# An attention-LSTM recurrence: 1/sum moved into the transposing product, and both gate products of a cell in one operation

## The reference

```python
def _lstm_cell(x, h, c, Wi, Wh, bi, bh):
    g = x @ Wi.T + bi + h @ Wh.T + bh
    i, f, gg, o = jnp.split(g, 4, axis=-1)
    c2 = jax.nn.sigmoid(f) * c + jax.nn.sigmoid(i) * jnp.tanh(gg)
    h2 = jax.nn.sigmoid(o) * jnp.tanh(c2)
    return (h2, c2)

def step(carry, x_t):
    h0, c0, h1, c1, a = carry
    xin = jnp.concatenate([x_t, a], axis=-1)
    h0, c0 = _lstm_cell(xin, h0, c0, Wi0, Wh0, bi0, bh0)
    h1, c1 = _lstm_cell(h0, h1, c1, Wi1, Wh1, bi1, bh1)
    q = h1 @ Wq.T
    attn = jax.nn.softmax(jnp.einsum('bh,bsh->bs', q, context), axis=-1)
    mixed = jnp.einsum('bs,bsh->bh', attn, context)
    a2 = jnp.tanh(jnp.concatenate([mixed, h1], axis=-1) @ Wo.T + bo)
    return ((h0, c0, h1, c1, a2), a2)
```

## Time and profile before

| | us |
|---|---|
| median of 3 runs | 1889.4 |
| lowest, highest | 1886.71, 1890.64 |
| the profiled execution | 1888.54 |
| its span, first to last instruction | 1886.8 |
| PE busy in the span | 1474.4 (78%) |
| DVE busy | 1174.6 (62%) |
| ACT busy | 760.2 (40%) |
| POOL busy | 207.7 (11%) |

### The profile page before, as it was taken

The page is one execution under the profiler, slowest core; times in us unless marked ns, Lnnn a source line. Parts: engine busy times, 40 slices in busy tenths (PEclk is TensorE's granted clock), DMA queues, the critical chain, the costliest instruction groups (busy, mean ns, idle before and its releaser), DMA issues. The chain is left out here.

```text
span 1886.8 us, 82660 instructions
## 1 busy us (share of the span) xinstructions
PE 1474.4 (78%) x34335; PEld 1282.6 (68%) x34336; DVE 1174.6 (62%) x4397; ACT 760.2 (40%) x1849; POOL 207.7 (11%) x427
## 2 busy tenths in 40 slices
PE   1557777777734999999999999999999783049997
PEld 0446666666623888888888888888888673026665
DVE  5878888888885556666666656666666484014444
ACT  2446666566554334444344444444344211013332
POOL 0000000000001000000000000000000002743333
PEclk9768888898856999999999999999999765569999
DMA  6000000000034000000000000000000160222222
GB/s 212 1 2 0 0 0 0 0 0 0 1 90 199 6 0 0 0 0 0 0 0 0 0 0 0 0 0 0 0 0 0 32 203 28 104 79 67 71 73 50
DMA packets 42813, 57.39 MB, mean 30 GB/s; under 512 B 5754, under 2 KB 32892, under 8 KB 40856
## 3 DMA queue, kind: packets, MB, share of 16 engines
q1 hardware_dynamic: 36672, 42.90, 7.5%
q0 software_dynamic: 5376, 12.66, 1.9%
q10 hardware_dynamic: 728, 1.34, 0.2%
HBM read 30.52 MB, written 26.88 MB: 30 GB/s over the span
## 5 line engine op out<-in xcount | busy, mean ns | idle before, releaser
L1517 DVE TENSOR_TENSOR hb<-psH,b_sb 128x512 f32<-128x512 f32 x72 | 49.8, 691 | 170.6 <-PE psH L1341 170.6
L900 PE MATMUL sc_a<-h_a,KH 128*128 128x48 f16 (+2 forms) x4096 | 124.2, 183 | 2.5 <-DVE h_a L1058 2.5
L900 PE MATMUL sc_b<-h_b,KH 128*128 128x48 f16 (+2 forms) x4096 | 123.0, 183 | 0.0
L860 PE MATMUL z_b<-h_b,WL 128*128 128x64 f16 x2304 | 112.2, 193 | 11.4 <-issue 3.0
L860 PE MATMUL z_a<-h_a,WL 128*128 128x64 f16 x2304 | 112.5, 194 | 9.3 <-DVE h_a L1050 1.8
L940 PEld LDWEIGHTS mx_a<-pmv_a,VH 128*128 128x128 f16 x4096 | 107.1, 96 | 16.4 <-DVE pmv_a L1086 16.1
L940 PEld LDWEIGHTS mx_b<-pmv_b,VH 128*128 128x128 f16 x4096 | 107.4, 96 | 15.9 <-DVE pmv_b L1086 15.9
L940 PE MATMUL mx_a<-pmv_a,VH 128*128 128x16 f16 x4096 | 113.2, 169 | 5.3 <-DVE pmv_a L1086 0.4
L940 PE MATMUL mx_b<-pmv_b,VH 128*128 128x16 f16 x4096 | 113.2, 170 | 5.0 <-DVE pmv_b L1086 0.3
L900 PEld LDWEIGHTS sc_a<-h_a,KH 128*128 128x128 f16 x4096 | 113.1, 96 | 2.6 <-DVE h_a L1058 2.6
L900 PEld LDWEIGHTS sc_b<-h_b,KH 128*128 128x128 f16 x4096 | 113.2, 96 | 0.0
(11 more groups left out here) (282 smaller groups left out, 3748.5 us busy)
## 6 DMA issues: line engine op xcount, KB each, us to landing
sorted_x<-zt SPq DMA_DIRECT2D x9, 1032.0 KB, 11.9
xr<-sorted_x SPq DMA_DIRECT2D x72, 65.0 KB, 1.8
xg<-sorted_x SPq DMA_DIRECT2D x72, 64.0 KB, 1.9
XT<-in_ctxT SPq DMA_DIRECT2D x1, 4096.0 KB, 13.1
x_scratch<-X SPq DMA_DIRECT2D x1, 4096.0 KB, 15.9
TOK<-x_scratch SPq DMA_DIRECT2D x4, 1024.0 KB, 10.2
w_sb<-in_w SPq DMA_DIRECT2D x1, 2048.0 KB, 12.8
b_sb<-in_b SPq DMA_DIRECT2D x1, 2048.0 KB, 19.8
```

The source lines that it names most:

```text
L860: mm = nc.tensor.matmul(q.z[layer][:, j * GB:(j + 1) * GB], WL[:, blk + j, w, :], mov[m], start=False, stop=False, skip_group_check=True)
L900: mm = nc.tensor.matmul(A.S[:, WIDE * n:WIDE * n + streamed(n)], KH[:, k, pair * P:(pair + 1) * P], A.h[1][:, 2 * n:2 * n + streamed(n) // ...
L1517: nc.vector.tensor_tensor(hb[:, u, :], psH[:, u, :], b1_sb[:, bass.ds(col, FF)], ALU.add).then_inc(v_hb, 1)
```

## The change

Three edits. The masked copy `pe` and its transposition are replaced: DVE writes two diagonal matrices, `dg[:, h, :]`, which are the constant `pick` (S at row s, column s where s has the parity h, else 0) times the reciprocal of each row; PE multiplies p, as the stationary operand of 64 x 64, with each of them and writes the two results to the lower and the upper 64 partitions. The first of the three own products is issued after the wait for `dg` and before this product; the other two stay where they were. The gate products: the cell state c becomes the fourth quarter of the gate tile, so that (i+1)g and (f+1)c are one operation of 128 columns. The tanh of the output gate gets a tile and an operation of its own, after the tanh of i, f, g. `pe`'s clearing is gone, and the count of the clearing semaphore is 16 instead of 18.

```diff
-                    nc.vector.tensor_reduce(par[:, 0:1], ident[0:64, 0:64:2], AX.X, ALU.add).then_inc(v_b, 1)
-                    nc.vector.tensor_reduce(par[:, 1:2], ident[0:64, 1:64:2], AX.X, ALU.add).then_inc(v_b, 1)
-                    dve.wait_ge(v_b, 3)
-                    nc.vector.tensor_scalar(pmask[:, :, :], par[:, :].unsqueeze(2).broadcast_to([64, 2, 64]),
-                                            S, None, ALU.mult).then_inc(v_b, 1)
+                    dve.memset(pick[:, :, :], 0.0).then_inc(v_b, 1)
+                    dve.wait_ge(v_b, 2)
+                    for h in range(2):
+                        nc.vector.tensor_scalar(pick[:, h, h::2], ident[0:64, h:64:2], S, None, ALU.mult).then_inc(v_b, 1)
...
                 q.gt = [sb(f"gt{l}_{t}", [P, 4, GB]) for l in range(2)]
+                q.c = [q.gt[l][:, 3, :] for l in range(2)]
+                q.og = [sb(f"og{l}_{t}", [P, GB]) for l in range(2)]
...
+                    def own_part(q, k):
+
+                        w, m = ((0, 0), (1, 0), (0, 1))[k]
+                        nc.tensor.matmul(q.Mv[:, :, :, 0], WO2[:, w, :],
+                                         q.h[1][:, 0:GB, m].rearrange("p (n b) -> p n b", b=2),
+                                         start=(k == 0), stop=False, skip_group_check=True)
...
-                            pe.wait_ge(A.s_pe, at + 1)
-                            nc.tensor.transpose(A.S[:, 128:256], A.pe[:, :], ident[:, :]).then_inc(A.s_pt, 1)
+                            pe.wait_ge(A.s_dg, at + 1)
+                            own_part(A, 0)
+                            for h in range(2):
+                                mm = nc.tensor.matmul(A.S[64 * h:64 * (h + 1), 128:192], A.p[:, :], A.dg[:, h, :],
+                                                      start=True, stop=True)
+                            mm.then_inc(A.s_pt, 1)
                             if not last:
                                 early0x(A, at + 1)
...
-                            for k, (w, m) in enumerate(((0, 0), (1, 0), (0, 1))):
-                                nc.tensor.matmul(A.Mv[:, :, :, 0], WO2[:, w, :],
-                                                 A.h[1][:, 0:GB, m].rearrange("p (n b) -> p n b", b=2),
-                                                 start=(k == 0), stop=False, skip_group_check=True)
+                            own_part(A, 1)
+                            own_part(A, 2)
...
-                            nc.scalar.activation(L.gt[l][:, :, :].rearrange("p g b -> p (g b)"), L.z[l][:, 0:4 * GB],
+                            nc.scalar.activation(L.gt[l][:, 0:3, :].rearrange("p g b -> p (g b)"), L.z[l][:, 0:3 * GB],
                                                  ACT.Tanh, scale=sc[:, I0 + l:I0 + l + 1]).then_inc(L.s_tg[l], 1)
+                            nc.scalar.activation(L.og[l][:, :], L.z[l][:, 3 * GB:4 * GB],
+                                                 ACT.Tanh, scale=sc[:, I0 + l:I0 + l + 1]).then_inc(L.s_to[l], 1)
...
-                            act.wait_ge(L.s_tg[l], lt + 1)
-                            nc.scalar.activation(L.os[l][:, :], L.gt[l][:, 3, :], ACT.Copy, scale=S / 2,
+                            act.wait_ge(L.s_to[l], lt + 1)
+                            nc.scalar.activation(L.os[l][:, :], L.og[l][:, :], ACT.Copy, scale=S / 2,
                                                  bias=S / 2).then_inc(L.s_os[l], 1)
...
-                        pool.memset(q.pe[:, :], 0.0).then_inc(s_zero, 1)
-                    pool.wait_ge(s_zero, 18)
+                    pool.wait_ge(s_zero, 16)
...
-                            nc.vector.scalar_tensor_tensor(L.u[l][:, 0, :], L.gt[l][:, 1, :], 1.0, L.c[l][:, :],
+                            nc.vector.scalar_tensor_tensor(L.u[l][:, :, :], L.gt[l][:, 0:2, :], 1.0, L.gt[l][:, 2:4, :],
                                                            ALU.add, ALU.mult).then_inc(L.s_uv[l], 1)
-                            nc.vector.scalar_tensor_tensor(L.u[l][:, 1, :], L.gt[l][:, 0, :], 1.0, L.gt[l][:, 2, :],
-                                                           ALU.add, ALU.mult).then_inc(L.s_uv[l], 1)
-                            dve.wait_ge(L.s_uv[l], 2 * lt + 2)
-                            nc.vector.scalar_tensor_tensor(L.c[l][:, :], L.u[l][:, 0, :], 0.5, L.u[l][:, 1, :],
+                            dve.wait_ge(L.s_uv[l], lt + 1)
+                            nc.vector.scalar_tensor_tensor(L.c[l], L.u[l][:, 1, :], 0.5, L.u[l][:, 0, :],
                                                            ALU.mult, ALU.add).then_inc(L.s_c[l], 1)
...
-                            nc.vector.scalar_tensor_tensor(
-                                A.pe[0:64, :].rearrange("p (h s) -> p h s", h=2),
-                                A.p[:, :].unsqueeze(1).broadcast_to([64, 2, 64]), A.r[:, 0:1], pmask[:, :, :],
-                                ALU.mult, ALU.mult).then_inc(A.s_pe, 1)
+                            nc.vector.tensor_scalar(A.dg[:, :, :], pick[:, :, :], A.r[:, 0:1], None,
+                                                    ALU.mult).then_inc(A.s_dg, 1)
```

More of the change, by code:

```diff
@@ L94, in decoder_kernel @@
         smask = sbr("smask", [P, 2 * GB])
-        pmask = sbr("pmask", [64, 2, 64])
+        pick = sbr("pick", [64, 2, 64])
         bo_sb = sbr("bo_sb", [P, 1])
@@ L125, in decoder_kernel @@
             tmp = sb("tmp", [P, 8])
-            par = sb("par", [64, 2])
             ktmp = sb("ktmp", [P, 2, 512])
@@ L776, in decoder_kernel @@
                 q.gt = [sb(f"gt{l}_{t}", [P, 4, GB]) for l in range(2)]
+                q.c = [q.gt[l][:, 3, :] for l in range(2)]
+                q.og = [sb(f"og{l}_{t}", [P, GB]) for l in range(2)]
                 q.u = [sb(f"u{l}_{t}", [P, 2, GB]) for l in range(2)]
-                q.c = [sb(f"c{l}_{t}", [P, GB]) for l in range(2)]
                 q.tc = [sb(f"tc{l}_{t}", [P, GB]) for l in range(2)]
@@ L790, in decoder_kernel @@
                 q.r = sb(f"r_{t}", [64, 1])
-                q.pe = sb(f"pe_{t}", [P, P])
+                q.dg = sb(f"dg_{t}", [64, 2, 64])
                 q.pm = sb(f"pmv_{t}", [P, GB + PADM, 2], F16)
@@ L811, in decoder_kernel @@
                 q.s_r = sem(f"r_{t}")
-                q.s_pe = sem(f"pe_{t}")
+                q.s_dg = sem(f"dg_{t}")
                 q.s_pm = sem(f"pm_{t}")
@@ L818, in decoder_kernel @@
                 q.s_tg = [sem(f"tg{l}_{t}") for l in range(2)]
+                q.s_to = [sem(f"to{l}_{t}") for l in range(2)]
                 q.s_tc = [sem(f"tc{l}_{t}") for l in range(2)]
@@ L853, in _ @@
                 def _(pe):
-                    pe.wait_ge(s_zero, 18)
+                    pe.wait_ge(s_zero, 16)
                     def gates(q, layer, blk, mov, parts=((0, 0), (1, 0), (0, 1))):
@@ L966, in cell_tanh @@
                             act.wait_ge(L.s_c[l], lt + 1)
-                            nc.scalar.activation(L.tc[l][:, :], L.c[l][:, :], ACT.Tanh, scale=0.5).then_inc(L.s_tc[l], 1)
+                            nc.scalar.activation(L.tc[l][:, :], L.c[l], ACT.Tanh, scale=0.5).then_inc(L.s_tc[l], 1)
                         if L:
@@ L995, in _ @@
                         for tile in (q.c[0], q.c[1]):
-                            pool.memset(tile[:, :], 0.0).then_inc(s_zero, 1)
+                            pool.memset(tile, 0.0).then_inc(s_zero, 1)
                         for k in range(2):
                             pool.tensor_copy(q.xs[:, k, :], XT[:, k, 0, q.g * GB:(q.g + 1) * GB]).then_inc(s_zero, 1)
-                        pool.memset(q.pe[:, :], 0.0).then_inc(s_zero, 1)
-                    pool.wait_ge(s_zero, 18)
+                    pool.wait_ge(s_zero, 16)
                     for q in G:
@@ L1031, in _ @@
                 def _(dve):
-                    dve.wait_ge(s_zero, 18)
+                    dve.wait_ge(s_zero, 16)
                     def half(L, A, lt, at):
```

## The result

The changed kernel takes 1923.6 us (median of 4 runs, 1922.1 to 1925.7), the kernel before 1888.2 over as many; the ratio is 1.0187 (95% interval 1.0169 to 1.0205). The forecast was 1904, with a range from 1886 to 1920: the direction is right, the size is not. The profiled execution took 1922.7 us, its span 1920.9 against 1886.8.

What follows compares the result with a forecast made beforehand. The slackless softmax chain up to the mixing products was taken to bound each half; 128 x 0.12 = 15.4 us, less 0.3, gave 1903.6, or 1904.5 against the median; predicted 1904, range 1886 to 1920.

Steps and rivals of the forecast that it cites:

- What bounds a half: Each half: one slackless chain from scores through softmax and pe to the mixing products sets its end; LSTM cell beside it.
- Fused gate product, output gate apart: LSTM cell: c 0.06 to 0.07 us earlier, i, f, g 0.05 earlier, added tanh hidden on ACT; worth 0.
- Diagonal: DVE writing dg instead of pe: 0.285 us against 0.34, same start, so ending 0.055 earlier.
- Own product and drain: PE after dg: the 64x64 product waits for the own product to drain at the shape change; +0.11 us a half.
- the second rival: PE after dg: own product costs nothing, cast at 1009.15, -0.01 us a half, 1888 us; chance 0.15.
- Product: The two 64x64 fp32 products on PE: column halves run side by side, 0.34 us (bounds 0.30 and 0.45).
- the serial rival: The product's two column halves run one after the other: 0.45 us, +0.23 a half, 1918 us; chance 0.16.
- Once only: Outside the loop: two memsets of pe gone from POOL, -0.3 us; the constant in the first stage, 0.
- the sum: Whole kernel: 128 x 0.12 = 15.4 us, less 0.3, gives +15.1, predicting 1904 us.
- other losses: Remaining chance, 0.03, for losses beyond the forecast and its named rivals; no place or size given.

Runs made afterwards that it cites:

- The cell's edits alone: Kernel before with only the fused gate products and the output gate's separate tanh: 1889.9 us, ratio 1.0005.
- the wait before pe alone: Kernel before with one more 64-column DVE operation, its result unused, ahead of pe, delaying the old transposition: 1918.4 us, ratio 1.0157.
- the own product late: Changed kernel with the first own product moved back behind the x gates, a PE semaphore increment carrying the wait for dg: 1903.4 us, ratio 1.0085.
- the filler: Changed kernel with six more 64-column products, into unread columns, where PE waits for the low part of pmv: 1905.6 us, ratio 1.0084.
- own product first: Kernel before with the first own product between the wait for pe and the old transposition, same array shape: 1892.8 us, ratio 1.0017.

## Why the prediction was wrong

- **What bounds a half**: right. The cell's edits alone moved the half by 0.01, the wait before pe alone by 0.14.
- **Fused gate product, output gate apart**: right, 0 us. u took 0.28, tanh of 192 columns 0.42, the added one 0.31, and ACT's queue was done before tanh c was due.
- **Diagonal**: 0.27 for 0.285.
- **Own product and drain**: right in mechanism; the total of 0.12 is right too, but its split is not. The product started 0.16 after the own product's start, where I had 0.15 for its load. By the second rival the cast should come 0.13 earlier without the own product, and the half should be 0.01 shorter than before. With the own product late the cast came 0.08 earlier (0.79 after the diagonal's start instead of 0.87), and the half was 0.05 longer than before. So the fit to the hundredth is in part luck.
- **Product**: 0.33 for 0.34, two halves side by side; the serial rival is out. The time was near that rival's 1918, by another cause. The Trainium skill's rule that a load overlaps a running matmul only in another row group (TensorE: Matmul & The Clock Gate, Part 3, What overlaps and what doesn't) doesn't hold here: rows equal, columns different, the four loads are through 0.19 after the start while the products run to 0.33, against 0.45 in one column group.
- **Once only**: not resolved. The first exp came at 607.9 instead of 606.4, in a stretch where the clock changes.
- **The step that failed is the sum**: 128 x 0.12 took all halves to be equal, and priced every PE row at the clock of 0.99 that the earlier trace rows shows. No term stood for what more waiting does to the clock, and "other losses" had a chance of 0.03. What came was 14 halves longer by 1.2 to 1.3 us. With the falls taken away by the filler, the same sum holds within 1.1 us.

The trace before had a sign of it. Where PE waits longer, at both ends of the loop, the clock is down (0.59 and 0.78):

```profile
560.00:607.00 47.00, 17.82 (x260) 14.23 (x260) 30.23 (x58) 23.38 (x20) 5.17 (x22) 0.59 0.36 147
1497.00:1886.80 389.80, 242.34 (x1408) 187.25 (x1405) 158.89 (x484) 76.86 (x168) 134.19 (x140) 0.78 0.29 86
```

It doesn't tell how far away a fall in the loop was, nor the price of 1.3 us for each, which only the runs gave. But a rival "the added wait costs the clock" should have stood.

## What to carry to other kernels

A wait added to a PE stream that is busy without a break elsewhere can have two prices, its length and the clock. Look at the distances of all iterations and not at one, and at the clock column over the loop; if some iterations are long and have a clock of half, try filler products in the wait before anything else. And keep narrow products away from wide ones that run just before them on the chain: put the wide ones behind, or let them end while the input is still being made, and look in the timeline whether they do: what stands ahead of them in the queue may hold them back.

## What the runs showed of the hardware

- The clock can fall in a loop that keeps PE busy for 97% of its time by the records: 14 falls in 922 us, each for some 3.4 us. They repeat at fairly even distances (58 to 65 us in the changed kernel), and the count is no smooth function of the half's length: none at 6.98 (own product first), 4 at 7.00, 12 at 7.02, 14 at 7.08 and none at 7.08 with filler, 7 at 7.10 with the old product, each in one profiled execution.
- Two fp32 products of 64 rows and 64 columns into different output halves took 0.33 us together; two into the same half, one after the other, 0.45 (the reshaping product, 128 rows).
- A load of another array shape starts 0.05 to 0.07 us before the running matmul's end, with the 64x64 shape (1010.72 against 1010.79, 999.73 against 999.78) as with 128x64. A product of the same shape started 0.04 after the running one (1004.44 after 1004.40, the old transposition).
